# First attention of a Flamingo block: the copy of a head's output and the closing of the head, each moved by one place in the software pipeline

## The reference, cut to what matters

```
q = _qdq(x) @ _qdq(wq).T + bq
k, v = split(cond @ wkv.T + bkv, 2, axis=-1)
attn = softmax(einsum('bnhd,bmhd->bhnm', q, k) * scale, axis=-1)
o = einsum('bhnm,bmhd->bnhd', attn, v)
```

## Time and profile before

| | |
|---|---|
| median of three runs | 3400.31 us |
| lowest and highest | 3397.11 and 3408.0 us |
| profiled execution, its own time | 3397.18 us |
| span from its first to its last instruction | 3395.5 us |
| mean granted clock of TensorE | 0.951 |
| busy over the span: PE, DVE, ACT, POOL | 2967.9, 2407.9, 2095.9, 1345.9 us |
| stage of the change in the span | about 205.5 to 591.3 us |
| units, heads in it | 256, 64 |

### The profile page before, as it was taken

One profiled execution on the slowest core, in us unless ns is written; L12 is line 12 of the kernel. 1 busy time (PEld: TensorE's weight loads), 2 busy tenths in 40 slices (PEclk: granted clock), 3 DMA queues, 4 the chain that ended last, 5 costly groups with the idle time before them and its releaser, 6 DMA issues. The chain is left out here.

```text
span 3395.5 us, 57647 instructions
## 1 busy us (share of the span) xinstructions
PE 2967.9 (87%) x15511; PEld 2362.9 (70%) x15542; DVE 2407.9 (71%) x4803; ACT 2095.9 (62%) x4247; POOL 1345.9 (40%) x1667
## 2 busy tenths in 40 slices
PE   6859898687999969859999969999999999899677
PEld 4636665475888858647777758888888888687444
DVE  6759998764667568746666259899999899525387
ACT  3458887331666546536666468888888888422254
POOL 3400000513000066235555257777777777331122
PEclk9979999897999989979999989999999999899899
DMA  5776553405778478754546532322222232476200
GB/s 181 242 167 150 147 144 97 135 35 192 261 256 281 157 236 248 186 152 136 171 142 183 178 111 93 93 91 93 83 82 86 92 93 67 141 253 204 73 22 28
DMA packets 403247, 490.88 MB, mean 145 GB/s; under 512 B 36388, under 2 KB 251828, under 8 KB 403092
## 3 DMA queue, kind: packets, MB, share of 16 engines
q1 hardware_dynamic: 391140, 440.31, 43.1%
q0 software_dynamic: 11952, 48.78, 4.1%
HBM read 312.69 MB, written 176.31 MB: 144 GB/s over the span
## 5 line engine op out<-in xcount | busy, mean ns | idle before, releaser
L2810 POOL TENSOR_SCALAR h_probs<-h_exp,h_rowsum_inv 128x512 f32<-128x512 f32 x512 | 357.9, 699 | 271.8 <-PE h_pT L2660 258.7
L2736 DVE TENSOR_REDUCE h_neg_max<-h_scores 128x1 f32<-128x512 f32 x512 | 349.4, 682 | 110.5 <-PE h_scores L2652 110.3
L2702 ACT ACTIVATE h_exp<-h_scores,h_neg_max 128x512 f32<-128x512 f32 x512 | 355.8, 695 | 113.8 <-DVE h_neg_max L2736 104.6
L2797 POOL TENSOR_TENSOR h_lo<-h_raw,h_hi 128x512 fp32r<-128x512 f32 x256 | 330.3, 1291 | 48.6 <-ACT h_hi L2691 48.6
L2749 DVE TENSOR_TENSOR h_probsT_lo<-h_pT,h_probsT_hi 128x512 fp32r<-128x512 f32 x512 | 348.6, 681 | 0.0
L2390 PE MATMUL g_pQ<-g_w_hi,g_x 128*128 (+1 forms) x640 | 275.1, 430 | 61.4 <-POOL g_w_lo L2513 60.0
L2660 PE MATMUL h_pT<-ident,h_probs 128*128 128x128 f32 x2048 | 306.8, 272 | 0.9 <-POOL h_probs L2810 0.8
L2660 PEld LDWEIGHTS h_pT<-ident,h_probs 128*128 128x128 f32 x2048 | 255.2, 141 | 69.0 <-POOL h_probs L2810 2.0
L2711 ACT CAST h_probsT_hi<-h_pT 128x512 fp32r<-128x512 f32 x512 | 301.1, 588 | 0.9 <-PE h_pT L2660 0.9
L2390 PE MATMUL g_pQ<-g_w_lo,g_x 128*128 (+1 forms) x640 | 260.3, 407 | 0.0
L2673 PE MATMUL h_pO<-h_probsT_hi,h_hi 128*128 128x512 f32 x512 | 244.5, 477 | 0.0
(11 more groups left out here) (418 smaller groups left out, 8347.4 us busy)
## 6 DMA issues: line engine op xcount, KB each, us to landing
e_w_raw<-in_w SPq DMA_DIRECT2D x24, 1792.0 KB, 7.7
lnT<-g_out SPq DMA_DIRECT2D x160, 256.0 KB, 2.3
h_raw<-lnT SPq DMA_DIRECT2D x64, 512.0 KB, 5.2
e_w_raw<-in_w SPq DMA_DIRECT2D x24, 896.0 KB, 9.7
b_q_stack<-qk SPq DMA_DIRECT2D x64, 256.0 KB, 7.0
b_k_stack<-qk SPq DMA_DIRECT2D x64, 256.0 KB, 8.9
xq<-f_out SPq DMA_DIRECT2D x16, 1024.0 KB
g_x<-xq SPq DMA_DIRECT2D x64, 256.0 KB, 2.9
```

What stands on the lines that cost most here:

```text
L2702: nc.scalar.activation(Pr[:, r % 4], pS[r % 2][:], ACT.Exp, bias=nmax[:, r % 4:r % 4 + 1], accum_out=rsum[:, r % 4:r % 4 + 1]).then_inc(ex ...
L2736: v.tensor_reduce(nmax[:, r % 4:r % 4 + 1], pS[r % 2][:], axis=AX, op=ALU.max, negate=True).then_inc(nmax_done.sem, 1)
L2797: nc.gpsimd.tensor_tensor(Lo[:, gb, slot], Raw[:, gb, slot], Hi[:, gb, slot], ALU.subtract).then_inc(op_lo.sem, 1)
L2810: nc.gpsimd.tensor_scalar(Pn[:, r % 4], Pr[:, r % 4], rinv[:, r % 4:r % 4 + 1], 1.0, ALU.mult, ALU.mult).then_inc(norm_done.sem, 1)
```

## The change

ACT's list begins with `o_copy`, whose lag goes from 9 to 10; DVE's `normalise` keeps its place behind `maxima` and its lag goes from 10 to 11. With that the copy of head h is in ACT's step 4h + 13 and the closing in DVE's step 4h + 14. Nothing else differs.

```diff
-            pipeline(act, N, 2 * UN, [(high, 3), (exps, 1), (o_copy, 9)])
+            pipeline(act, N, 2 * UN, [(o_copy, 10), (high, 3), (exps, 1)])
...
-            pipeline(dve, N, 2 * UN, [(low, 4), (maxima, 0), (normalise, 10)])
+            pipeline(dve, N, 2 * UN, [(low, 4), (maxima, 0), (normalise, 11)])
```

## The result

| | before | changed |
|---|---|---|
| median of 11 runs | 3398.16 us | 3415.3 us |
| lowest, highest | 3394.85, 3408.0 | 3405.01, 3418.73 |
| ratio, 95% interval | | 1.0047 (1.0038 to 1.0057) |
| profiled execution, span | 3397.18, 3395.5 | 3414.78, 3413.1 |
| stage, first scores to last product | 385.44 us | 402.60 us |

The changed kernel is 17 us slower. So the stage holds practically all of it.

What follows compares the result with a forecast made beforehand. The ring of PE and ACT bounds the kernel, DVE just 0.10 us behind. Terms 14.3 (62 x 0.23), 1.6 and 0.7 sum to 16.6 us slower: 3413.8 profiled, 3416.9 as median; range 3407 to 3426.

Steps and rivals of the forecast that it cites:

- The ring of PE and ACT: First attention: output transposes, transposes, cast, exp, output copy, values, output transposes again; sets the pace at 5.83 us per head.
- DVE's 0.10 of slack: Kernel before: the exp could have started at 374.19, not 374.29, so DVE has 0.10 us to spare per head.
- The 0.30 of the loop's turn: DVE's loop turn: lower half starts 0.50 behind the product, not 0.20; 0.10 of that was hidden before.
- ACT's half worth 0: Output copy moved to the head of ACT's next step: same instruction sequence, so cost 0.
- The wait that goes and the one that comes: DVE's reduce stops waiting for output transposes; its maximum waits for scores instead, making each head 0.23 us longer, 6.06.
- The two small terms: Costs DVE's 0.10 had hidden: 16 x 0.10 = 1.6 us at groups' first heads, 7 x 0.10 = 0.7 at loop turns.
- The first heads of groups: Their product also waits for the store, starting 0.56 behind the reduce, not 0.46: 0.10 x 16 = 1.6 us.
- The loops' turns: Lower half at DVE's loop turn starts later behind the product; 0.10 no longer hidden, x 7 = 0.7 us.
- A: DVE is the pace and every head's reduce loses its wait: 15.4 us off, 3385; chance 0.08.
- B: DVE's longer road covers the 0.84 us lost per loop turn: 10.7 or 8.2 slower, 3411 or 3408.5; chance 0.17.
- C: DVE pays the 0.84 us per loop turn once more: 5.9 on top, 22.5 slower, 3423; chance 0.12.
- D: The change to ACT's and DVE's lists does nothing: 3400; chance 0.03.

Runs made afterwards that it cites:

- the closing at lag 12: DVE's normalise at lag 12, still behind the maximum, against the changed kernel's lag 11: median 3387.51 us, ratio 0.9989 to the kernel before, stage 380.50 us.

## Why the prediction was right

*The size.* 16.6 us were forecast, 17.1 measured; 3417 forecast against the median of 3400.31 then at hand, and 3415.3 measured beside one of 3398.16. The mechanism was right; that the sum came this near is in part luck, since of its three terms two were too low and one too high, as shown below.

*The ring of PE and ACT as the pace.* Right. Taking the exp out of it (copy between cast and exp) gave 7.6 us of stage beyond what the closing at lag 12 gave, with DVE's work untouched. The same edit with the closing still at lag 10 was not run.

*DVE's 0.10 of slack.* Right, as far as the traces test it. One head in eight has a product 0.10 later behind its reduce than the others, in both kernels. It is the closing of the earlier trace rows; here are the output transposes before and after it in the kernel before, and then the same head in the changed kernel:

```profile
412.09 0.46 PE L802 MATMUL b_pR<-ident,b_oT 64*128 64x64 f32 x4
...
417.92 0.46 PE L802 MATMUL b_pR<-ident,b_oT 64*128 64x64 f32 x4
```

```profile
420.55 0.46 PE L802 MATMUL b_pR<-ident,b_oT 64*128 64x64 f32 x4
...
422.67 0.42 DVE L865 TENSOR_REDUCE b_o_sum<-b_pR 128x128 f32<-128x256 f32 x1
423.22 0.29 DVE L869 TENSOR_TENSOR b_o<-b_o_sum,b_rowsum_inv 128x128 f32<-128x128 f32 x1
...
426.71 0.46 PE L802 MATMUL b_pR<-ident,b_oT 64*128 64x64 f32 x4
```

Before, that head takes 5.83 like any plain one, so the 0.10 is hidden; changed, it takes 6.16 where plain ones take 6.08, so most or all of it is paid. That is a lower bound of the slack. The 0.30 of the loop's turn is not hidden whole (5.96 in place of 5.83), so there is less than that to spare. The added reciprocal of 0.06 tells the same, though of the kernel with lag 12 and not of the kernel before: hidden there, paid in full behind the change.

*ACT's half worth 0.* Right, shown by that half alone.

*The wait that goes and the one that comes.* Right in place and in size. The price of the scores was taken as 0.51 and is 0.52 (377.79 to 378.31). The maximum was to come 0.41 later than a DVE that never waits would start it (0.60 behind the start of the lower half); in the head shown it comes 0.42 later, which the profile, counting from the end of the lower half (377.29 + 0.69), notes as 0.33. The plain heads, 62 at 0.23 by the sum (14.3 us), are 61 at 0.24 to 0.26 (some 15 us).

*The two small terms.* Their sum is near what was forecast (2.3 us), but neither of them is. The first heads of groups were sized too high: the late product is there in the first head of every second group only, and it grows by 0.34 (5.82 to 6.17 in most), so 7 x 0.10 = 0.7 us in place of 16 x 0.10 = 1.6. (The kernel before already showed it in seven heads only; why every second group is open.) The loops' turns were sized too low: the two long heads there went from 6.38 and 5.96 to 6.74 and 6.32, each by 0.36, which is the plain 0.25 and 0.11 more; one 0.10 was forecast for the two, so 1.5 us in place of 0.7. The head just ahead of the longer one grew by only 0.22, which takes some 0.2 us back.

*The rivals.* A (DVE is the pace) fell with its own wait gone and the time longer; and the kernel with lag 12 ahead of the maximum has no wait of the reduce and is slower too. B (turns swallowed) fell: the two long heads there are longer by more than the plain ones, not less. Its account of the 0.84 was incomplete as well: in the head of 6.38 the transposes wait 0.33 for DVE, not for PE or ACT. C (added up once more, 0.84 per eight heads) fell: about 0.2 per eight heads were added. D holds for ACT's half alone. The price of a compare-and-branch that the Trainium skill gives ("Advanced Engine Details and Errata", section Control Flow Timing) would have hidden nearly all of a turn; the trace sides with the row's 0.30, since the head behind which DVE's loop turns grew by 0.11 more than a plain one.

*The rule of the most-contended engine.* By the rule of the Trainium skill ("Perfetto Trace Analysis", Identifying the Most-Contended Engine) DVE was to be seen to first. It was the busiest engine, and yet the change that took away its one large wait lost time. After the ring had been loosened at another engine, DVE did become the pace. Here the rule points at the right engine one step too early.

## What to carry to other kernels

Where several engines are each nearly full, find the ring: follow one unit from an instruction back to the same instruction of the next unit, and note for every engine beside the ring how much later it could be. An instruction group moved to kill a wait must not land between a late arrival and something that the ring needs; here the same three instructions cost 17 us behind one maximum and brought 3.8 us of stage ahead of it, 4.9 one step later (both of them where a bank is reused after two steps and where the loop turns, not in the plain heads). And the instruction in front of a copy that frees a single buffer is on the ring, even if it has nothing to do with it: moving the copy ahead of the exp brought 7.6 us, more than the best place of the closing did.

## What the runs showed of the hardware that was not expected

A loop that jumps back over 96 steps costs far more than one over 32: 3.25 us of idle time on DVE against 0.21, 3.5 on PE, with no releaser in the profile, and then, after PE had stood still, a granted clock of 0.65 on the mean of 6.4 us, between its two levels (1.2 and 2.4 GHz). With a lag of DVE that differs from PE's the two stalls come one after the other. The Trainium skill, "Runtime: NRT & Kernel Launch", section Instruction fetch mechanics, says that a taken branch to code outside a small window makes the sequencer fetch it first. The two lengths of idle time agree with that in kind, but no run here varied the length of the code alone, so the cause stays open.
